# Graph attention over sixteen graphs: four of each moved group's sixteen SBUF transfers go from SyncE's queue to GpSimd's

## What is computed

```python
q = (x @ Wq + bq).reshape(b, m, h, d)      # b=16, m=1024, h=8, d=64
k = (x @ Wk + bk).reshape(b, m, h, d)
v = (x @ Wv + bv).reshape(b, m, h, d)
scores = einsum('bmhd,bnhd->bhmn', q, k) / sqrt(d) + edge_bias[adj]
scores = leaky_relu(scores, 0.2)
attn = softmax(where(adj > 0, scores, -1e9), axis=-1)
x = layernorm(x + einsum('bhmn,bnhd->bmhd', attn, v).reshape(b, m, h * d) @ Wp + bp)
```

## Time and profile before

| | |
|---|---|
| median of 3 runs | 8837.18 us (8823.2 to 8840.01) |
| profiled execution | 8834.99 us, its span 8833.2 us |
| busy share of the span | PE 90%, DVE 84%, ACT 80%, POOL 16% |
| chain of waits by engine | PE 37%, SP's queue 22%, DVE 15%, issue 13%, ACT 10% |
| moved by the DMA engines | 822.72 MB, 93 GB/s on average |
| mean granted clock of PE | 0.965 |

### The profile page before, as it was taken

One profiled execution on the slowest core, in us unless ns is written; L12 is line 12 of the kernel. 1 busy time (PEld: TensorE's weight loads), 2 busy tenths in 40 slices (PEclk: granted clock), 3 DMA queues, 4 the chain that ended last, 5 costly groups with the idle time before them and its releaser, 6 DMA issues.

```text
span 8833.2 us, 166143 instructions
## 1 busy us (share of the span) xinstructions
PE 7962.8 (90%) x58440; PEld 3499.7 (40%) x58440; DVE 7408.1 (84%) x11192; ACT 7043.3 (80%) x8220; POOL 1428.6 (16%) x582
## 2 busy tenths in 40 slices
PE   3898998989989898998989989999898998989999
PEld 2433435344353433534334343343534435343342
DVE  3788887988879888798888988889788887988888
ACT  2788787987869878798787887878788787987877
POOL 0301203021030210303012030120302103021000
PEclk7899999999999999999999999999999999999999
DMA  2614426144161532626235171441614416153250
GB/s 69 163 37 107 113 55 159 40 120 97 50 158 47 134 77 65 147 50 147 60 79 135 45 171 37 104 116 50 166 38 118 101 49 159 47 132 78 60 126 19
DMA packets 430043, 822.72 MB, mean 93 GB/s; under 512 B 163874, under 2 KB 221218, under 8 KB 427042
## 3 DMA queue, kind: packets, MB, share of 16 engines
q1 hardware_dynamic: 429090, 810.76, 38.1%
HBM read 76.25 MB, written 4.19 MB: 9 GB/s over the span
## 4 chain that ended last, share of the span: by engine, by line
PE 37%; SPq 22%; DVE 15%; issue 13%; ACT 10%; DMA 1%; DVEq 0%; ACTq 0%; POOL 0%; POOLq 0%
SPq L393 22%; PE psum L837 21%; ACT work L1064 6%; DVE work L1426 5%; PE psum L619 3%; PE psum L541 2%; PE psum L536 2%; DVE work L1304 2%; DVE work L1276 2%; PE psum L714 2%; PE psum L555 1%; PE psum L689 1%; PE psum L804 1%; ACT spare L906 1%; ACT spare L901 1%
## 5 line engine op out<-in xcount | busy, mean ns | idle before, releaser
L837 PE MATMUL psum<-work,pick 128*32 128x512 f32 x32768 | 3766.0, 599 | 204.8 <-DVE work L1426 157.7
L1064 ACT ACTIVATE work<-spare,ucol 128x1024 f32<-128x1024 f32 x3402 | 3632.9, 1145 | 52.2 <-PE psum L837 47.8
L1426 DVE TENSOR_SCALAR work<-spare,ucol 128x1024 f32<-128x1024 f32 x4790 | 3251.3, 748 | 71.8 <-PE psum L837 56.0
L837 PEld LDWEIGHTS psum<-work,pick 128*32 128x32 f32 x32768 | 976.9, 110 | 2545.1 <-issue 2062.6
L974 ACT ACTIVATE work<-psum,beta 128x1024 f32<-128x1024 f32 x1024 | 1140.2, 1113 | 450.8 <-PE psum L689 346.0
L1304 DVE STREAM_TRANSPOSE work<-work 128x1024 f32<-128x1024 f32 x960 | 1191.1, 1241 | 235.7 <-DMA work<-work 130.2
L1276 DVE CUSTOM_DVE_ANT_0 work<-psum,work 128x1024 f32<-128x1024 f32 x1024 | 1223.6, 1195 | 146.1 <-ACT work L974 136.9
L981 ACT ACTIVATE work<-work,least 128x1024 f32<-128x1024 f32 x1024 | 1173.3, 1146 | 34.5 <-DVE least L1276 34.5
L1507 POOL TENSOR_TENSOR rstd<-rstd,neg_half 128x8 f32<-128x8 f32 x64 | 131.5, 2055 | 4959.6 <-DVE rstd L1214 4959.6
L685 PE MATMUL psum<-mask,ident_b 128*128 128x512 bf16 x2048 | 636.4, 393 | 254.2 <-DVE least L1276 249.9
L689 PE MATMUL psum<-x_split,q_hi 128*128 128x512 f32 x2048 | 851.0, 497 | 0.0
(11 more groups left out here) (179 smaller groups left out, 7136.5 us busy)
## 6 DMA issues: line engine op xcount, KB each, us to landing
work<-work SPq DMA_DIRECT2D x2560, 128.0 KB, 2.4
spare<-work SPq DMA_DIRECT2D x1280, 128.0 KB, 2.7
adj_in<-in_adj SPq DMA_DIRECT2D x128, 512.0 KB, 5.1
q_lo<-adj_in SPq DMA_DIRECT2D x1024, 64.0 KB, 2.0
q_lo<-spare SPq DMA_DIRECT2D x1024, 64.0 KB, 2.0
work<-work SPq DMA_DIRECT2D x1792, 32.0 KB, 1.8
mask<-mask_next SPq DMA_DIRECT2D x16, 2048.0 KB, 9.2
x_in<-in_x SPq DMA_DIRECT2D x16, 256.0 KB, 9.6
```

Of the source, the lines that this page charges most:

```text
L837: mm = pe.matmul(slot[32 * q:32 * q + 32, cols], pick[:, 15 - kk:47 - kk], ring[kk % 4][q][:, cols], start=False, stop=(kk == 15), skip_gr ...
L1064: ins = act.activation(ring[kk % 4][q], v3, ACT.Relu, bias=ucol[:, 4 * T + q, kk:kk + 1])
L1426: ins = dve.tensor_scalar(ring[kk % 4][q], v3, ucol[:, 4 * T + q, kk:kk + 1], 0.0, ALU.add, ALU.max)
```

## The change

SP issues the first three of the four turns of a group in layer 2, 12 transfers. POOL's queue issues the fourth turn, 4 transfers, in the new function `move_rest`, after the same waits as SP's. They count on semaphores of their own (`s_moved_rest`), for which PE's `pv_quad` and DVE's `turn_tile` wait besides the old ones. In POOL's `layer2` a loop over the 15 groups now sets the order: the group's transfers, then, after groups 0, 1, 3, 4, 6, 9, 11 and 12, a conversion, and after groups 7 and 11 and at the end an `add_pair`. Block moves of the other layers stay as they were.

```diff
@@ -54,6 +54,8 @@
 GROUPS = NT * 16
 KEEP = 16
 MOVE_DONE = 16 * 16
+SP_DONE = 12 * 16
+REST_DONE = 4 * 16
 SPAN = 63
 
 HIS_A = 5
@@ -302,6 +304,7 @@
         s_probs = sem("s_probs")
         s_blocks = sem("s_blocks")
         s_moved = [sem(f"s_quad_moved{i}") for i in range(4)]
+        s_moved_rest = [sem(f"s_quad_moved_rest{i}") for i in range(4)]
         s_pv = sem("s_pv")
         s_copied = sem("s_copied")
         s_hi = sem("s_hi")
@@ -385,9 +388,9 @@
 
             ADJ_AFTER = {2: (2,), 3: (3,), 4: (4,), 8: (5,), 10: (6,), 11: (7,)}
 
-            def move(dst, src, done):
+            def move(dst, src, done, turns=4):
                 parts = src.rearrange("p (c y) -> p c y", c=4)
-                for turn_ in range(4):
+                for turn_ in range(turns):
                     for a in range(4):
                         c = (a + turn_) % 4
                         sp.dma_start(dst[32 * c:32 * c + 32, a, :], parts[32 * a:32 * a + 32, c, :]).then_inc(done, 16)
@@ -408,7 +411,7 @@
                     dst = quadT[k % 3].rearrange("p (a y) -> p a y", a=4)
                     if k == 2 and tail is not None:
                         store(tail)
-                    move(dst, blocks[k % 2], s_moved[k % 4])
+                    move(dst, blocks[k % 2], s_moved[k % 4], 3)
                     if more:
                         for t in ADJ_AFTER.get(k, ()):
                             next_adj(g + 1, t)
@@ -705,7 +708,8 @@
                         pe.wait_ge(s_copied3, tail * 2 + 2)
                     if k == 2:
                         pe.wait_ge(s_beta4, g + 1)
-                    pe.wait_ge(s_moved[k % 4], g * (MOVES[k % 4] * MOVE_DONE) + (moved_before(k) + 1) * MOVE_DONE)
+                    pe.wait_ge(s_moved[k % 4], g * (MOVES[k % 4] * SP_DONE) + (moved_before(k) + 1) * SP_DONE)
+                    pe.wait_ge(s_moved_rest[k % 4], g * (MOVES[k % 4] * REST_DONE) + (moved_before(k) + 1) * REST_DONE)
                 src = quadT[k % 3].rearrange("p (a b h x) -> p b a h x", a=4, h=2, x=F)
                 cols = slice(2 * tt * P, 2 * tt * P + 2 * P)
                 for j in range(part_ * NT // 2, (part_ + 1) * NT // 2):
@@ -1296,8 +1300,9 @@
             def turn_tile(g, it, n):
                 k, half, h, moved = in_quad(n)
                 if moved and k >= 2 and half == 0 and h == 0:
-                    dve.wait_ge(s_moved[(k - 2) % 4],
-                                g * (MOVES[(k - 2) % 4] * MOVE_DONE) + (moved_before(k - 2) + 1) * MOVE_DONE)
+                    r, count = (k - 2) % 4, moved_before(k - 2) + 1
+                    dve.wait_ge(s_moved[r], g * (MOVES[r] * SP_DONE) + count * SP_DONE)
+                    dve.wait_ge(s_moved_rest[r], g * (MOVES[r] * REST_DONE) + count * REST_DONE)
                 if moved:
                     dve.wait_ge(s_probs, g * TILES2 + n + 1)
                     dst = blocks[k % 2].rearrange("p (c b h t i) -> p c b h t i", c=4, h=2, t=2, i=32)
@@ -1523,33 +1528,56 @@
                 largest(g)
                 inverse_deviation(s_var_a, s_rstd_a, g * 2 + 2)
 
-            def layer2(g, it, more):
+            def move_rest(g, k, tail):
+                filled_ = pool.to_reg(g * 4 * MOVED + 4 * k + 4)
+                free = pool.to_reg(g * QUADS + k - 2) if k >= 3 else None
+                before = None if tail is None else pool.to_reg({0: tail * NT + NT, 2: tail * 2 + 2}.get(k, 1))
+                pool.wait_ge(s_setup, SETUP)
+                pool.wait_ge(s_blocks, filled_)
+                if free is not None:
+                    pool.wait_ge(s_pv, free)
+                if k == 0 and tail is not None:
+                    pool.wait_ge(s_pv3, before)
+                if k == 2 and tail is not None:
+                    pool.wait_ge(s_xn3, before)
+                pool.wait_ge(s_setup, SETUP)
+                to = quadT[k % 3].rearrange("p (a y) -> p a y", a=4)
+                parts = blocks[k % 2].rearrange("p (c y) -> p c y", c=4)
+                for a in range(4):
+                    c = (a + 3) % 4
+                    pool.dma_start(to[32 * c:32 * c + 32, a, :], parts[32 * a:32 * a + 32, c, :])\
+                        .then_inc(s_moved_rest[k % 4], 16)
+
+            CONVERTED_AFTER = {0: 0, 1: 1, 3: 2, 4: 3, 6: 4, 9: 5, 11: 6, 12: 7}
+
+            def layer2(g, it, more, tail):
                 pool.wait_ge(s_xn_a, g * 4 + 4)
                 pool.tensor_tensor(acc[:], xdup[:, :, 0, :], bp_b[:].unsqueeze(1).to_broadcast([P, NT, F]), ALU.add)\
                     .then_inc(s_acc, 1)
-                for pair in range(HP):
-                    if more:
-                        if pair == 0:
-                            copied = pool.to_reg(g * 16 + 16)
-                            pool.wait_ge(s_setup, SETUP)
-                            pool.wait_ge(s_mask, copied)
-                        for t in ((0, 1, 2), (3, 4, 5), (6, 7), ())[pair]:
-                            convert(g + 1, g * CONV + 3, t)
-                    if pair + 1 < HP:
-                        add_pair(g, it, pair)
+                if more:
+                    copied = pool.to_reg(g * 16 + 16)
+                    pool.wait_ge(s_setup, SETUP)
+                    pool.wait_ge(s_mask, copied)
+                for k in range(MOVED):
+                    move_rest(g, k, tail)
+                    if more and k in CONVERTED_AFTER:
+                        convert(g + 1, g * CONV + 3, CONVERTED_AFTER[k])
+                    if k % 4 == 3 and k > 4:
+                        add_pair(g, it, k // 4 - 1)
+                add_pair(g, it, HP - 2)
 
             ahead(0)
-            layer2(0, first, True)
+            layer2(0, first, True, None)
             with pool.Fori(0, B - 2) as g:
                 inverse_deviation(s_var2, s_rstd2, g + 1)
                 ahead(g + 1)
                 inverse_deviation(s_var3, s_rstd3, g + 1)
-                layer2(g + 1, body(g), True)
+                layer2(g + 1, body(g), True, g)
             inverse_deviation(s_var2, s_rstd2, B - 1)
             ahead(B - 1)
             inverse_deviation(s_var3, s_rstd3, B - 1)
             pool.sem_inc(s_mask_next, 1)
-            layer2(B - 1, body(B - 2), False)
+            layer2(B - 1, body(B - 2), False, B - 2)
             inverse_deviation(s_var2, s_rstd2, B)
             inverse_deviation(s_var3, s_rstd3, B)
```

## The result

| | before | with the change |
|---|---|---|
| median (range) of 4 runs each | 8831.72 us (8823.2 to 8840.01) | 8993.12 us (8987.31 to 9008.82) |
| ratio, 95% interval | | 1.019 (1.0175 to 1.0205) |
| profiled execution: time, span | 8834.99, 8833.2 us | 8987.31, 8985.5 us |
| mean granted clock of TensorE | 0.965 | 0.953 |

The change costs 161 us, where +239 was forecast: slower, and inside the range.

A forecast was written before the change was run, and what follows sets the result against it. SP's full issue queue was taken to set DVE's pace, with PE, DVE, ACT and DMA near full. Per round +17.2 us, with first and last rounds +247 on 8835.0, shaded by 10 us: 9074 us, range 8860 to 9230.

The forecast's parts named there:

- The price of POOL's issue: POOL's time to issue one block transfer in layer 2: 1.0 us, bounds 0.59 and 1.29.
- Step 1: Head of the round: POOL issues group 0's transfers behind rstd and `acc`, so DVE's group 2 starts 6.4 us late.
- Step 2: Conversions on POOL ahead of groups 1 and 2's transfers make DVE wait another 2.1 and 4.2 us.
- Step 3: Later groups: after the conversions behind 3 and 4, group 5's transfers land 1.8 us late; other conversions cost nothing.
- Step 4: ACT's copies wait for POOL's `add_pair`: 9.8 us behind group 11 and its conversion, 2.9 us after group 7.
- Step 5: Relief of SP's queue shortens DVE's waits for moves from group 4 on: -10 us per round, bounds 0 and -16.8.
- The sum: All layer 2 terms: +17.2 us per round, +241 in 14 rounds, first round +5, last +1.
- Cheap issue: Rival: POOL issues at SP's 0.59 us, so a smaller loss, +6.2 us per round, 8925 us; chance 0.25.
- The dear issue: Rival: POOL's issue takes 1.29 us, so +30 us per round, 9260 us; chance 0.13.
- The DMA engines as the limit: Rival: a second issuer brings no bytes faster, 7 of 10 us relief fall away, 9175 us; chance 0.07.
- SP was all that mattered: Rival: POOL issues at 0.59 us, relief is 16.8, ACT's copy waits for free: faster, 8712 us; chance 0.09.
- The signs named: Trace signs: DVE waits 5 to 8 us, then two shorter; ACT some 10 us once a round; SP pauses.

The follow-up runs named there:

- e1_head: The change with POOL's rstd of layer 3 and start of `acc` behind the transfers of groups 0 and 1: 8888.87 us.
- e2_add_first: The change with `add_pair` behind group 11 ahead of that group's conversion: 8897.66 us.
- e3_both: The change with the edits of e1_head and e2_add_first together: 8806.54 us, ratio 0.9961 to the kernel before.
- e6_order_add: The change with SP issuing all 16 transfers, POOL keeping the new order, and `add_pair` ahead of the conversion: ratio 1.0003 to the kernel before.
- e8_eight: e3_both with eight transfers of a group on POOL in place of four: 8870.16 us, ratio 1.0042 to the kernel before.
- e5_spread: e3_both with conversions behind groups 0, 1, 3, 5, 7, 9, 11, 13 and some adjacency loads earlier: 8777.15 us, ratio 0.9946 to the kernel before.
- e7_two: e3_both with two transfers of a group on POOL in place of four: 8777.89 us, ratio 0.9937 to the kernel before.
- e9_spread_two: e5_spread with two transfers of a group on POOL in place of four: 8772.74 us, ratio 0.9931 to the kernel before.
- e10_spread_eight: e5_spread with eight transfers of a group on POOL in place of four: 8796.97 us, ratio 0.9953 to the kernel before.

## Why the prediction was right, and where its sizes were off

**The direction and the two mechanisms: right.** The head's wait and ACT's stall at `add_pair` were named as the main terms, and e1_head and e2_add_first took each away by itself: 104 and 95 us, together 200; e3_both took 187 (by the ratios 112, 110 and 202). e6_order_add shows that nothing else in the order costs.

**The price of POOL's issue: wrong, 1.0 us against 0.49.** I chose it nearest to the all-reduce of one column. The nearer row was SP's 0.59 us for the same transfer, the lower of my bounds, and POOL is below even that. The landing after the last issue was too short by as much in all: 2.0 us assumed, 3.99 measured in the round read. I had carried SP's landing over to POOL.

**Step 1, the head: 6.4 forecast, 6.21 measured in the round read, 6.3 as a median.** Right for two wrong reasons. Issue and landing were put at 0.3 + 4.0 + 2.0 = 6.3 us; the rows show 2.19 us of issues and 3.99 more until DVE starts (2484.84 to 2491.02). The errors cancel here, because the wait runs to the landing.

**Step 2, 2.1 and 4.2 us for the next groups: not there.** They hang on POOL's issue time, which adds up from group to group. The conversion begins at 2487.11, group 1's four are out at 2498.8, and DVE's first tile of group 3 does not wait. The 2.77 us at group 4 stand where 2.22 stood before, and are for SP's transfers of group 2, as before: in the middle rounds the last of them lands 13.9 us after the group is full, POOL's last after 12.8. The stretch 8-16 is 24.6 us against 24.8.

**Step 3, +1.8 us for the later pair: not there.** DVE's first tile of group 7, which needs group 5's move, does not wait in the middle rounds (median 0). 16-48 as a whole is 2.0 us less.

**Step 4, ACT's stall: 9.8 + 2.9 forecast, 7.0 measured.** The first is 7.58 us in the round read, less by 2.2 us, which is the issue price again (2.06 us for four in place of 4.3). The second, after group 7, did not occur: ACT waits 15 times, once a round. It rested on POOL being 3 us late from the conversion behind group 6; it came 1.2 us after group 7 was full (median), and with the cheap issue the add is in time. With eight transfers it appears, 2.2 us a round (e8_eight). Not in the sum was TensorE's clock, which falls to half behind the stall.

**Step 5, the relief: -10 forecast, -2.0 measured in groups 4 to 12, and -3.0 in e3_both.** This is the term that was furthest off. I counted 12 issues as 12 x 0.65 + 0.3 = 8.1 us; in the trace they take 7.65 to 10.35, and a landing is 1.0 us longer on SP and 1.7 on POOL. Neither was in the sum. And I took the waits as one pool that fewer issues drain: those of groups 4 and 5, 4.9 us of the round before (medians 2.8 and 2.1), did not shrink (2.9 and 2.7), since SP's last transfer of groups 2 and 3 lands as late as before: 13.9 and 15.7 us after the group is full, 13.6 and 15.2 before. I had drawn the size from the last round, which has no adjacency loads on SP; but neither has it conversions on POOL, nor the loads' bytes on the DMA engines, and a round that differs in three things is no price for one. What paces groups 4 to 12 at about 87 to 88 us in all the good versions was not tried apart. From group 6 to 12 DVE hardly waits for a move any more, so it is not SP there; before groups 4 and 5 it still is.

**The sum:** 12.7 + 1.8 + 12.7 - 10 = 17.2 us per round forecast, 6.3 - 0.2 + 7.0 - 2.0 - 0.8 = 10.3 measured. The first round came close to the forecast (+5, measured 5.9), the last less so (+1, measured 2.6). That the total still lies in the range is in part luck: the two stalls and what follows them were put at 27.2 us and came to 13.1, the relief at 10 and came to 2.8, and the two errors work against each other.

**The rivals.** Cheap issue (8925 us) had the right price and, with my relief of 10, too small a loss; with its own 16.2 us and the measured relief of 2.0 it would have said +14. The dear issue is out. The DMA engines as the limit: its result, that most of the relief falls away, is what happened, by slower landings and a stretched SP queue. The mean share fell from 0.89 to 0.83, but in the stretch shown in which both queues issue it is 0.96 at 251 GB/s, so this rival is not refuted, and no run varied the bytes. That SP was all that mattered: out as the change stands, yet e3_both, e5_spread, e7_two, e9_spread_two and e10_spread_eight are faster by 0.4 to 0.7%. The gain is there once the two stalls are gone, and is some 2 to 4 us per round, not 16.8.

**The signs named.** Right: a DVE wait of 5 to 8 us behind rstd of layer 3 (6.21), one ACT wait a round, pauses in SP's queue. Not as named: two shorter waits behind the first, and POOL's issues at 1.0 us.

## What to carry to other kernels

When a queue is relieved by a compute engine, price first what stands in front of the moved step in that engine's program, and who waits for what now stands behind it: here two such places cost 200 us, while the relief was worth 35. Place first and share second: transfers ahead of anything that waits, short work that others wait for ahead of long work that nobody does, and then no more transfers than the relief needs (of sixteen, two did better than four and four than eight in e3_both's order; in the spread order two and four are not told apart). An issue time saved is not a transfer made faster, so count issue to landing under both queues.

## What the runs showed of the hardware

- POOL issues a move of 32 partitions (128 KB) in 0.49 us, SP in 0.59, while the all-reduce of one column, the shortest computation of POOL that I had priced, took 1.15 us. The gap between four of POOL's in a row is small: 2.06 us for four.
- With a second issuer the median landing gets longer: SP's from 2.4 us alone to 3.1, 3.5 and 4.0 with 2, 4 and 8 of 16 on POOL. It is a matter of the moment: with the change, SP's transfers of the middle rounds land after 2.4 us where no transfer of POOL is under way, and after 4.1 where one is. POOL's first of a group lands after 3.4 us, each later one later.
- SP's issues stay at 0.59 us at the median, but some take 1.4 to 1.8 us while POOL's transfers are under way. Group 0 shows it, with POOL's four 20 us later (the change, first line) and beside them (e1_head, second line). What causes it the traces do not show.

```profile
2465.21 7.53 SPq L396 DMA_DIRECT2D work<-work  x12
```

```profile
2433.89 9.58 SPq L396 DMA_DIRECT2D work<-work  x12
```

- While both queues had transfers under way, the DMA engines moved some 236 GB/s, with SP's alone 201: the single transfer was slower and the sum of them faster.
- TensorE stood for 8.18 us, and its granted clock fell to 0.50 and was back only some 5 us after it had started again; the same 16 matmuls took 2.91 us in place of 1.95.
- Moving one engine's four transfers shows up as another engine's wait two steps on: POOL's add 7.58 us late, ACT's copy with it, DVE's `leaky` 7.92 us late. Over the run DVE's wait for ACT is the largest of them (318.4 us), and the one that causes its growth is much smaller (115.1).
